# A two-layer graph kernel: scores of a block row from its diagonal block on, the other blocks as PE transposes of kept score blocks

## The chip, the cores and the metric

The kernel runs on one core of a Trainium2 chip. A core has a matrix engine (TensorE, in the profile PE for matmuls and PEld for the weight loads that precede them), a vector engine (VectorE, DVE), a scalar engine (ScalarE, ACT), GpSimd (POOL) and a sync engine (SP) that issues DMAs here. Each engine runs its own instruction stream in order and they meet at semaphores. The metric is the device time of one execution in microseconds (us). Before the change the median of three runs is 462.99 us (461.92 to 464.63).

## The reference, cut to what matters

Eight batches (B = 8) of N = 1024 nodes with H = 128 features, all f32, and an adjacency matrix `adj` of 0 and 1 per batch.

```python
# layer 0
u = einsum('bnh,bmh->bnm', x, x) / 128 ** 0.5      # symmetric in n and m
scores = softmax(u, axis=-1)
delta = scores * adj
att = delta / (sum(delta, axis=2, keepdims=True) + 1e-10)
# att is split in the parts right of, on and left of the diagonal, each with its own projection
ctx = att_left @ (x @ Wl.T + bl) + att_self @ (x @ Ws.T + bs) + att_right @ (x @ Wr.T + br)
x = layernorm(x + relu(ln_w * norm(ctx) + ln_b))
# layer 1
d = (sum(adj, axis=-1) + 1e-5) ** -0.5
x = layernorm(x + (d[:, :, None] * adj * d[:, None, :]) @ (x @ W1) + b1)
```

`u` is symmetric: block (i, j) of 128 x 128 is the transpose of block (j, i).

## The kernel before, in words

A batch is cut into NB = 8 block rows of P = 128 nodes (HB = 4 is half of them). Per batch and block row i the work goes round the engines like this:

- PE `scores(b, i)`: the block row of `u`, 128 x 1024, into the PSUM buffer `ps_u` (two banks, one buffer for all block rows). x is held as a rounded part `xT_hi` and a rest `xT_lo` (dtype float32r), and `split_matmul` multiplies hi by hi, hi by lo and lo by hi, each over 512 columns, twice: six matmuls (lines 403 to 405, printed with `ps_u` as output).
- DVE `row_max` (line 1060) reduces `ps_u` to the negative row maximum; ACT `exps` (line 805) writes exp(u - max) from `ps_u` to `d_rows` in SBUF. `scores` of the next block row waits for `exp_done`, since it overwrites `ps_u`.
- DVE `masked` (line 1067) multiplies with the adjacency rows; PE `turn_d` (line 463) makes eight 128 x 128 transposes into `ps_d`; ACT `d_out` (line 812) copies them to `dT`; POOL `masks` (line 1405) cuts the diagonal block; PE `context_far` and `context_near` (lines 478 and 484) multiply with the projected rows `h_sum`.

Beside them per batch: eight projections of x on PE (`project`, 384 columns each, lines 403 to 405 with `ps_m` as output) with a bias add on DVE (line 263); DVE 32 x 32 transposes of the adjacency (`turn_blocks`) that DMAs from SP complete into `aT`; the second layer's products `gather` (line 498, 512 columns, into `ps_y`), a copy `y_out` to `yT` on ACT (line 850) and `second_product` (line 510); the layer norms, spread over DVE, POOL and ACT. `x1b` holds the residual rows with the bias of layer 1 and `fin` the result rows before the store. ACT sums adjacency rows with a copy to `junk` whose accumulator is kept (line 818).

The order of the work on each engine is written out by hand, instruction by instruction: one list for batches 0 and 1 (`first_batches`), one for batches 2 to 6 (`batch(b, p)`, with p = b - 1 whose layers 0 and 1 finish inside batch b) and one for batch 7 and the end (`last_batches`). No planner or pool decides anything. Batch b's scores calls stand among the contexts, projections and gathers of batches b and p.

Of the kernel before, what the change touches and what calls it, by code (L numbers as in the profile page):

```python
# [11 lines left out]
P = 128  # L12
# [13 lines left out]
def two_layer_graph_kernel(nc, x, adj, Wl, bl, Ws, bs, Wr, br, ln_w, ln_b, W1, b1, out):  # L26
# [10 lines left out]
    with ExitStack() as ctx:  # L37
# [6 lines left out]
        def sem(name):  # L44
            return ctx.enter_context(nc.semaphore(name))
# [15 lines left out]
        x_turned = sb("x_turned", [P, NQ, NB, Q])  # L61
        h_sum = sb("h_sum", [P, 2, NB, 3 * H])
# [13 lines left out]
        junk_d = sb("junk_d", [P, P], mybir.dt.bfloat16)  # L76
# [45 lines left out]
        exp_done = sem("exp_done")  # L122
        d_ready = sem("d_ready")
# [90 lines left out]

        def y_bank(b, i0, i1):
# [52 lines left out]
        def _(sp):  # L268
# [58 lines left out]
            def first_batches(b, p):  # L327
# [26 lines left out]
                next_a(b, 1)
                next_a(b, 2)
                move_rows(b)
                next_a(b, 3)
                move_blocks(b, 0)
                next_a(b, 4)
                store(p, 0, HB)  # L360
                next_a(b, 5)
                next_a(b, 6)
                store(p, HB, NB)

            def batch(b, p):
# [12 lines left out]
                next_a(b, 5)
                store(p, HB, NB)
                next_a(b, 6)  # L380

            def last_batches(b, p):

                move_blocks(p, 1)
                next_a(p, 7)
# [7 lines left out]

# [6 lines left out]
        def _(pe):  # L400
# [34 lines left out]
            def scores(b, i):  # L435
# [68 lines left out]
            def second_product(b, i0, i1):  # L504
# [4 lines left out]
                for i in range(i0, i1):  # L509
                    last = pe.matmul(o_bank(b, i0, i1)[:, i - i0, :], yT[:, i * P:(i + 1) * P],  # L510
# [3 lines left out]
            def first_batches(b, p):  # L514
# [80 lines left out]
                gather(p, 0, HB, 3, 4)  # L595
# [12 lines left out]
                gather(p, 0, HB, 4, 8)  # L608
# [18 lines left out]
            def batch(b, p):  # L627
# [31 lines left out]
                gather(p, 0, HB, 3, 4)  # L659
# [9 lines left out]
                gather(p, 0, HB, 4, 8)  # L669
# [6 lines left out]
                gather(p, HB, NB, 1, 4)  # L676
# [3 lines left out]
                gather(p, HB, NB, 4, 8)  # L680
# [8 lines left out]
            def last_batches(b, p):  # L689
# [29 lines left out]
                gather(p, 0, HB, 2, 4)  # L719
# [17 lines left out]
                gather(p, 0, HB, 4, 6)  # L737
                gather(p, 0, HB, 6, 8)
# [15 lines left out]
                gather(p, HB, NB, 2, 4)  # L754
                gather(p, HB, NB, 4, 6)
                gather(p, HB, NB, 6, 8)
                m_read_o(p, 0, HB)
                second_product(p, HB, NB)
                gather(b, 0, HB, 0, 4)
                gather(b, HB, NB - 2, 0, 2)  # L760
                gather(b, NB - 2, NB, 0, 2)
                gather(b, 0, HB, 4, 6)
                gather(b, 0, HB, 6, 8)
# [3 lines left out]
                gather(b, HB, NB - 2, 3, 4)  # L767
                gather(b, HB, NB - 2, 4, 6)
                gather(b, HB, NB - 2, 6, 8)
                gather(b, NB - 2, NB, 2, 4)  # L770
                second_product(b, HB, NB - 2)
                gather(b, NB - 2, NB, 4, 6)
                gather(b, NB - 2, NB, 6, 8)
                second_product(b, NB - 2, NB)

# [31 lines left out]

# [811 lines left out]
```

## Time and profile before

| | |
|---|---|
| runs, median (lowest to highest) | 462.99 us (461.92 to 464.63) |
| span of the profiled execution | 461.6 us (the profile has no other time for it) |
| PE / PEld busy | 444.2 / 357.7 us |
| DVE / ACT / POOL busy | 388.8 / 296.8 / 310.9 us |
| score matmuls on `ps_u`, L403 + L404 + L405, x372 | 154.1 us busy |
| transposes L463, x512 | 66.4 us busy |
| exp on ACT, L805, x62 | 68.9 us busy, 50.3 us idle before them |

Matmuls are pipelined: the time of one (mean 394 ns for a 512-column score matmul) is longer than the distance to the next one's start, so it is the distance between starts that tells what it costs in a row. The number in brackets at a row's end is the idle time of the engine before it and what ended it.

### The profile page before, as it was taken

To read this page: it belongs to the slowest core of one execution; us is meant where nothing else is said; L and a number is where in the kernel's file an instruction comes from. 1 tells how busy PE (TensorE), PEld (TensorE's weight loads), DVE (VectorE), ACT (ScalarE), POOL (GpSimd) and SP (SyncE) were. 2 spreads that over 40 slices of the span, in tenths; PEclk is the share of its full clock that TensorE was granted. 3 is DMA by queue.
4 is the path that set the end of the run, shared out by engine and by line. 5 is a ranking of instruction groups with operands and counts; after the bars stand their busy time and mean duration, and the time that the engine had idled before them with its cause. 6 is when DMAs were issued, how large, how long until landed. Compare 5 with 4: busy or idle time off the path is not lost. (4 is left out here: it accounts for less than half of the span.)

```text
span 461.6 us, 8799 instructions
## 1 busy us (share of the span) xinstructions
PE 444.2 (96%) x2663; PEld 357.7 (77%) x2663; DVE 388.8 (84%) x696; ACT 296.8 (64%) x611; POOL 310.9 (67%) x364
## 2 busy tenths in 40 slices
PE   6899999999999999999999999999999999999974
PEld 4689879589776988679786797769887697879453
DVE  2998899979999889988899889998899887988625
ACT  2768767666666766765767657676676667677320
POOL 2115767379758867588675886588675967889662
PEclk9999999999999999999999999999999999999988
DMA  5836758285773889259881779528893493367721
GB/s 176 288 139 176 236 132 266 58 210 182 168 225 95 207 259 243 83 143 260 201 241 39 186 229 227 189 74 212 253 220 129 120 240 127 69 161 175 176 62 45
DMA packets 68878, 79.88 MB, mean 173 GB/s; under 512 B 7232, under 2 KB 60608, under 8 KB 68832
## 3 DMA queue, kind: packets, MB, share of 16 engines
q1 hardware_dynamic: 68768, 79.26, 62.1%
q8 instruction: 22, 0.36, 0.4%
q14 instruction: 24, 0.20, 0.1%
q0 software_dynamic: 64, 0.07, 0.0%
HBM read 38.40 MB, written 4.19 MB: 92 GB/s over the span
## 5 line engine op out<-in xcount | busy, mean ns | idle before, releaser
L478 PE MATMUL ps_c<-h_sum,dT 128*128 128x128 f32 x896 | 110.5, 275 | 0.9 <-issue 0.9
L478 PEld LDWEIGHTS ps_c<-h_sum,dT 128*128 128x128 f32 x896 | 106.9, 192 | 4.6 <-issue 4.0
L1405 POOL TENSOR_TENSOR dM<-dT,parts 128x384 f32<-128x384 f32 x64 | 67.9, 1063 | 58.2 <-ACT junk_d L826 31.7
L498 PE MATMUL ps_y<-aT,x1p 128*128 128x512 f32 x224 | 104.3, 592 | 0.0
L805 ACT ACTIVATE d_rows<-ps_u,nmax 128x1024 f32<-128x1024 f32 x62 | 68.9, 1112 | 50.3 <-DVE nmax L1060 50.2
L812 ACT ACTIVATE dT<-ps_d 128x1024 f32<-128x1024 f32 x64 | 65.3, 1021 | 40.8 <-PE ps_d L463 35.1
L1060 DVE TENSOR_REDUCE nmax<-ps_u 128x1 f32<-128x1024 f32 x62 | 75.3, 1215 | 16.6 <-PE ps_u L405 15.8
L1067 DVE CUSTOM_DVE_ANT_0 d_rows<-d_rows,a_rows 128x1024 f32<-128x1024 f32 x64 | 84.8, 1326 | 0.4 <-ACT d_rows L805 0.4
L1074 DVE STREAM_TRANSPOSE a_blk<-a_rows 128x1024 f32<-128x1024 f32 x64 | 77.4, 1228 | 0.8 <-DMA a_rows<-in_adj_dram 0.8
L818 ACT ACTIVATE junk<-a_rows 128x1024 bf16<-128x1024 f32 x64 | 67.1, 1048 | 0.3
L463 PE MATMUL ps_d<-parts,d_rows 128*128 128x128 f32 x512 | 66.4, 273 | 0.0
L463 PEld LDWEIGHTS ps_d<-parts,d_rows 128*128 128x128 f32 x512 | 58.6, 141 | 6.2 <-issue 4.4
L498 PEld LDWEIGHTS ps_y<-aT,x1p 128*128 128x128 f32 x224 | 39.7, 190 | 29.9 <-issue 29.4
L403 PE MATMUL ps_u<-xT_hi 128*128 128x512 f32 x124 | 56.6, 457 | 0.5
L405 PE MATMUL ps_u<-xT_hi,xT_lo 128*128 128x512 f32 x124 | 48.9, 394 | 0.0
L404 PE MATMUL ps_u<-xT_lo,xT_hi 128*128 128x512 f32 x124 | 48.6, 392 | 0.0
L263 DVE TENSOR_TENSOR h_sum<-ps_m,bias_bc 128x384 f32<-128x384 f32 x64 | 35.3, 551 | 14.7 <-PE ps_m L405 12.4
L484 PEld LDWEIGHTS ps_c<-h_sum,dM 128*128 128x128 f32 x256 | 36.0, 191 | 4.5 <-issue 2.9
L484 PE MATMUL ps_c<-h_sum,dM 128*128 128x128 f32 x256 | 38.9, 274 | 0.0
L255 POOL TENSOR_SCALAR fin<-fin,power_f,shift_f 128x128 f32<-128x128 f32 x56 | 36.2, 659 | 0.3
L1421 POOL TENSOR_TENSOR power_c<-var_c,minus_half 128x4 f32<-128x4 f32 (+1 forms) x17 | 22.2, 1304 | 20.1 <-DVE nmean_c L1119 20.1
L403 PE MATMUL ps_m<-wT_hi,xT_hi 128*128 128x384 f32 x64 | 28.4, 444 | 5.0 <-DVE h_sum L263 3.7
(95 smaller groups left out, 692.1 us busy)
## 6 DMA issues: line engine op xcount, KB each, us to landing
a_rows<-in_adj_dram SPq DMA_DIRECT2D x64, 512.0 KB, 4.5
aT<-a_blk SPq DMA_DIRECT2D x224, 128.0 KB, 2.9
x_rows<-in_x_dram SPq DMA_DIRECT2D x8, 512.0 KB, 4.5
a_rows<-a_blk SPq DMA_DIRECT2D x32, 128.0 KB, 2.4
out_dram<-fin SPq DMA_DIRECT2D x15, 256.0 KB, 2.6
x_turned<-x_blk SPq DMA_DIRECT2D x96, 32.0 KB, 1.9
out_dram<-fin SPq DMA_DIRECT2D x2, 128.0 KB, 1.8
fin<-in_L_gnn_Wl_dram SPq DMA_DIRECT2D x1, 64.0 KB, 3.4
```

Of the source, the lines that this page charges most:

```text
L403: pe.matmul(o, hi_l, hi_r, start=True, stop=False)
L463: last = pe.transpose(ps_d[:, j, :], d_rows[:, g % 3, j * P:(j + 1) * P], ident)
L478: pe.matmul(ps_c[:, c_place(b, i), :], dT[:, i % 2, j, :], h_sum[:, b % 2, j, k * H:(k + 1) * H], start=t == 0, stop=False)
L484: last = pe.matmul(ps_c[:, c_place(b, i), :], dM[:, i % 2, k, :], h_sum[:, b % 2, i, k * H:(k + 1) * H], start=False, stop=k == 1)
L498: last = pe.matmul(y_bank(b, i0, i1), gathered(b)[:, j, :], turned(b)[:, i0:i1, :, j, :].rearrange("p i q c -> p (i q) c"), start=j == 0, ...
L805: act.activation(d_rows[:, g % 3, :], u_bank(b, i), ACT.Exp, bias=nmax[:, i % 2:i % 2 + 1], accum_out=zsum[:, i:i + 1]).then_inc(exp_done, 1)
L812: act.activation(dT[:, i % 2, :, :], ps_d[:, :, :], ACT.Copy).then_inc(dt_out, 1)
L818: act.activation(junk[:, :], a_rows[:, i, :], ACT.Copy, accum_out=deg[:, i:i + 1])\
L1060: dve.tensor_reduce(nmax[:, i % 2:i % 2 + 1], u_bank(b, i), AX.X, ALU.max, negate=True)\
L1067: dve.tensor_tensor_reduce(out=d_rows[:, g % 3, :], in0=d_rows[:, g % 3, :], in1=a_rows[:, i, :], scale=1.0, scalar=0.0, op0=ALU.mult, op1 ...
L1074: dve.transpose(a_blk[:, i, :, :, :], a_rows[:, i, :].rearrange("p (j m c) -> p m j c", m=NQ, c=Q))\
L1405: pool.tensor_tensor(dM[:, i % 2, :, :], dT[:, i % 2, i, :].rearrange("p (a c) -> p a c", a=1).to_broadcast([P, 3, P]), parts[:, :, :], AL ...
```

## The change

In batch 0 nothing changes for the scores. From batch 1 on, `scores(b, i)` computes only the columns from block i on with `split_matmul`; blocks 0 to i - 1 of the row are PE transposes of blocks (j, i), j < i, which ACT has copied from `ps_u` to a new SBUF buffer `kept` when block row j stood there. The copy is `keep(b, j)` (one or two `Copy` activations), placed directly behind `exps(b, j)` for j = 0 to 6. `scores(b, i)` waits for the `keep` of the row before in addition to `exp_done`. To make room in SBUF, `yT` holds half of the rows, `x1b` lives in `fin` (in the last batch in a part of `h_sum`), and the junk outputs are 8 bits wide. Some neighbouring gather calls are merged into one call. All other orders are unchanged.

```diff
+        kept = sb("kept", [P, HB, HB, P])
-        yT = sb("yT", [P, N])
+        yT = sb("yT", [P, HB, P])
-        x1b = sb("x1b", [P, NB, H])
-        junk = sb("junk", [P, N], mybir.dt.bfloat16)
+        junk = sb("junk", [P, N], mybir.dt.float8e4)
...
+        def halves(b):
+            return b == 0
+
+        def kept_before(b, i):
+            return (NB - 1) * (b - 1) + i
+
+        def kept_parts(i):
+            if i == 0:
+                return [(kept[:, 0:2, :, :].rearrange("p a c m -> p (a c) m")[:, 1:NB, :], 1, NB)]
+            if i < HB - 1:
+                return [(kept[:, 0, 0:2, :] if i == 1 else kept[:, 0, 2:3, :], i + 1, HB), (kept[:, i + 1, :, :], HB, NB)]
+            if i == HB - 1:
+                return [(kept[:, 0, :, :], HB, NB)]
+            return [(kept[:, 1:NB - i, i - HB, :], i + 1, NB)]
...
             def scores(b, i):
...
-                for k in range(2):
-                    c = slice(k * HALF, (k + 1) * HALF)
-                    last = split_matmul(u_bank(b, i)[:, c], hi[:, s], lo[:, s], hi[:, c], lo[:, c])
+                if not halves(b) and i:
+                    pe.wait_ge(u_kept, kept_before(b, i))
+                j0 = 0 if halves(b) else i
+                for c in (slice(j0 * P, HALF), slice(max(j0 * P, HALF), N)):
+                    if c.start < c.stop:
+                        last = split_matmul(u_bank(b, i)[:, c], hi[:, s], lo[:, s], hi[:, c], lo[:, c])
+                for j in range(j0):
+                    last = pe.transpose(ps_u[:, j * P:(j + 1) * P], kept_block(j, i), ident)
                 last.then_inc(u_ready, 1)
...
+            def keep(b, i):
+                act.wait_ge(nmax_ready, NB * b + i + 1)
+                for v, j0, j1 in kept_parts(i):
+                    last = act.activation(v, ps_u[:, j0 * P:j1 * P].rearrange("p (j c) -> p j c", c=P), ACT.Copy)
+                last.then_inc(u_kept, 1)
...
             def rows_with_bias(b, i0, i1):
                 n, blk = NB * b + i1, slice(i0, i1)
                 pool.wait_ge(x_power, n)
-                wait(pool, o_read, NB * (b - 1) + HB * ((i1 - 1) // HB + 1))
+                if b == B - 1:
+                    pool.wait_ge(ctx_done, NB * b)
+                else:
+                    wait(pool, fin_free[i0 // HB], 16 * b)
+                x1b = rows_x1b(b)
```

On PE, block row 3 of a middle batch before the change (the projection in front of it fills `ps_m`, L498 with `ps_y` is a gather):

```order
L498 MATMUL ps_y<-aT,x1p 128x512
L403 MATMUL ps_u<-xT_hi 128x512 [waits exp_done,xt_split]
L404 MATMUL ps_u<-xT_lo,xT_hi 128x512
L405 MATMUL ps_u<-xT_hi,xT_lo 128x512
L403 MATMUL ps_u<-xT_hi 128x512
L404 MATMUL ps_u<-xT_lo,xT_hi 128x512
L405 MATMUL ps_u<-xT_hi,xT_lo 128x512
L403 MATMUL ps_m<-wT_hi,xT_hi 128x384 [waits xt_split,h_added]
```

The same place after the change (L433 to L435 are the old L403 to L405, L479 are the transposes of kept blocks, `parts` holds the identity, L533 is the gather):

```order
L533 MATMUL ps_y<-aT,x1p 128x512
L433 MATMUL ps_u<-xT_hi 128x128 [waits u_kept,exp_done,xt_split]
L434 MATMUL ps_u<-xT_lo,xT_hi 128x128
L435 MATMUL ps_u<-xT_hi,xT_lo 128x128
L433 MATMUL ps_u<-xT_hi 128x512
L434 MATMUL ps_u<-xT_lo,xT_hi 128x512
L435 MATMUL ps_u<-xT_hi,xT_lo 128x512
L479 MATMUL ps_u<-parts,kept 128x128 x3
L433 MATMUL ps_m<-wT_hi,xT_hi 128x384 [waits xt_split,h_added]
```

The first half of the row shrinks to one block of 128 columns and three transposes follow the second half; the first score matmul waits for `u_kept` too, and nothing else moves.

On ACT, block rows 0 and 1 of the same batch before the change (L812 is `d_out`, L826 the sum of the diagonal, L818 the adjacency row sum):

```order
L812 ACTIVATE dT<-ps_d 128x1024 [waits dt_tr,ctx_done]
L805 ACTIVATE d_rows,zsum<-ps_u,nmax 128x1024 [waits c_sum,dt_tr,nmax_ready]
L826 ACTIVATE junk_d,ddiag<-dM 128x128 [waits self_done,diag_done,mask_done] x2
L805 ACTIVATE d_rows,zsum<-ps_u,nmax 128x1024 [waits c_sum,dt_tr,nmax_ready]
L818 ACTIVATE junk,deg<-a_rows 128x1024 [waits a_in0,deg_added,deg_done]
```

And after it (L844, L831, L859 and L850 are the same four, L837 is `keep`):

```order
L844 ACTIVATE dT<-ps_d 128x1024 [waits dt_tr,ctx_done]
L831 ACTIVATE d_rows,zsum<-ps_u,nmax 128x1024 [waits c_sum,dt_tr,nmax_ready]
L837 ACTIVATE kept<-ps_u 128x896 [waits nmax_ready]
L859 ACTIVATE junk_d,ddiag<-dM 128x128 [waits self_done,diag_done,mask_done] x2
L831 ACTIVATE d_rows,zsum<-ps_u,nmax 128x1024 [waits c_sum,dt_tr,nmax_ready]
L837 ACTIVATE kept<-ps_u 128x256 [waits nmax_ready]
L837 ACTIVATE kept<-ps_u 128x512
L850 ACTIVATE junk,deg<-a_rows 128x1024 [waits a_in0,deg_added,deg_done]
```

One or two copies stand behind each exp and push what follows on ACT back.

## Rows read from the trace of the kernel before

**Rows 1.** The page, busy time of each engine, share of the span.

```profile
PE 444.2 (96%) x2663; PEld 357.7 (77%) x2663; DVE 388.8 (84%) x696; ACT 296.8 (64%) x611; POOL 310.9 (67%) x364
```

**Rows 2.** By stretch: length, busy PE, PEld, DVE, ACT, POOL, then PE clock, DMA.

```profile
42.00:101.40 59.40, 58.75 (x371) 48.30 (x370) 53.95 (x95) 41.77 (x87) 38.84 (x41) 1.00 0.64 180
264.40:318.70 54.30, 54.24 (x331) 43.89 (x330) 48.01 (x86) 36.83 (x77) 39.46 (x45) 1.00 0.67 187
```

**Rows 3.** Timeline, PE, 264.3 to 286 (batch 5): start, duration, instruction.

```profile
270.29 0.39 PE L403 MATMUL ps_u<-xT_hi 128*128 128x512 f32 x1
...
271.68 0.60 PE L484 MATMUL ps_c<-h_sum,dM 128*128 128x128 f32 x4
...
274.74 0.39 PE L403 MATMUL ps_u<-xT_hi 128*128 128x512 f32 x1
...
279.92 0.40 PE L404 MATMUL ps_u<-xT_lo,xT_hi 128*128 128x512 f32 x1
...
281.07 0.33 PE L403 MATMUL ps_m<-wT_hi,xT_hi 128*128 128x384 f32 x1
...
281.59 1.03 PE L463 MATMUL ps_d<-parts,d_rows 128*128 128x128 f32 x8
282.46 1.02 PE L498 MATMUL ps_y<-aT,x1p 128*128 128x512 f32 x2
...
283.50 0.34 PE L404 MATMUL ps_m<-wT_lo,xT_hi 128*128 128x384 f32 x1
...
283.85 1.02 PE L498 MATMUL ps_y<-aT,x1p 128*128 128x512 f32 x2
...
285.24 0.39 PE L404 MATMUL ps_u<-xT_lo,xT_hi 128*128 128x512 f32 x1
```

**Rows 4.** Timeline, 286 to 300, ACT's exp of block row 4, PE's scores of 5.

```profile
290.46 1.11 ACT L805 ACTIVATE d_rows<-ps_u,nmax 128x1024 f32<-128x1024 f32 x1
...
293.08 0.40 PE L404 MATMUL ps_u<-xT_lo,xT_hi 128*128 128x512 f32 x1
```

**Rows 5.** Timeline, ACT, 264.3 to 286, the exps of block rows 0 to 3.

```profile
268.86 1.11 ACT L805 ACTIVATE d_rows<-ps_u,nmax 128x1024 f32<-128x1024 f32 x1
...
273.14 1.11 ACT L805 ACTIVATE d_rows<-ps_u,nmax 128x1024 f32<-128x1024 f32 x1 [2.20 <-DVE nmax L1060]
...
277.58 1.11 ACT L805 ACTIVATE d_rows<-ps_u,nmax 128x1024 f32<-128x1024 f32 x1 [0.66 <-DVE nmax L1060]
...
283.58 1.11 ACT L805 ACTIVATE d_rows<-ps_u,nmax 128x1024 f32<-128x1024 f32 x1 [0.93 <-DVE nmax L1060]
284.59 0.19 ACT L805 ACTIVATION_READ_ACCUMULATOR d_rows<-ps_u,nmax 128x1 f32 x1
```

**Rows 6.** Groups by form: count, busy us, mean ns, idle before us.

```profile
L478 PE MATMUL ps_c<-h_sum,dT 128*128 128x128 f32 x896 | 110.5, 275 | 0.9 <-issue 0.9
...
L850 ACT ACTIVATE yT<-ps_y 128x512 f32<-128x512 f32 x15 | 9.0, 597 | 27.2 <-issue 20.1 <-PE ps_y L498 7.1
...
L850 ACT ACTIVATE yT<-ps_u 128x256 f32<-128x256 f32 x2 | 0.8, 383 | 6.1 <-PE ps_u L498 6.1
```

**Rows 7.** Timeline, 60 to 67 (batch 1): exp of block row 3, second score matmul of 4.

```profile
63.57 1.10 ACT L805 ACTIVATE d_rows<-ps_u,nmax 128x1024 f32<-128x1024 f32 x1
...
65.72 0.39 PE L404 MATMUL ps_u<-xT_lo,xT_hi 128*128 128x512 f32 x1
```

**Rows 8.** Timeline, 376 to 394 (batch 7): exps of 0 and 2, scores of 1, 3.

```profile
376.92 1.12 ACT L805 ACTIVATE d_rows<-ps_u,nmax 128x1024 f32<-128x1024 f32 x1 [2.46 <-DVE nmax L1060]
...
378.34 0.48 PE L403 MATMUL ps_u<-xT_hi 128*128 128x512 f32 x1
...
387.18 1.11 ACT L805 ACTIVATE d_rows<-ps_u,nmax 128x1024 f32<-128x1024 f32 x1 [0.68 <-DVE nmax L1060]
...
388.63 0.39 PE L403 MATMUL ps_u<-xT_hi 128*128 128x512 f32 x1
```

**Rows 9.** Timeline, PE, 408 to 462, the last batch's gather behind its moves.

```profile
440.59 2.74 PE L498 MATMUL ps_u<-a_rows,h_sum 128*128 128x256 f32 x8 [2.24 <-DMA a_rows<-a_blk]
```

More of the change, by code:

```diff
@@ L658, in batch @@
                 project(b, 7)
-                gather(p, 0, HB, 3, 4)
+                gather(p, 0, HB, 3, HB)
                 scores(b, 4)
@@ L668, in batch @@
                 turn_d(b, 3)
-                gather(p, 0, HB, 4, 8)
+                gather(p, 0, HB, HB, NB)
                 scores(b, 6)
@@ L675, in batch @@
                 turn_d(b, 4)
-                gather(p, HB, NB, 1, 4)
+                gather(p, HB, NB, 1, HB)
                 context_far(b, 3)
@@ L817, in degree @@
                 act.wait_ge(a_in[i], 16 * (b + 1))
-                act.activation(junk[:, :], a_rows[:, i, :], ACT.Copy, accum_out=deg[:, i:i + 1])\
+                act.activation(junk[:, :], a_rows[:, i, :], ACT.Copy, accum_out=deg[:, i:i + 1],
+                               saturate=False)\
                    .then_inc(deg_done, 1)
@@ L848, in y_out @@
                 act.wait_ge(y_done, NB * b + i1)
-                wait(act, o_ready, NB * (b - 1) + i1)
-                act.activation(yT[:, i0 * P:i1 * P], y_bank(b, i0, i1), ACT.Copy).then_inc(yT_ready, i1 - i0)
+                wait(act, o_ready, NB * b + (HB if i0 >= HB and b < B - 1 else 0))
+                if b == B - 1 and i0 >= HB:
+                    act.wait_ge(u_ready, NB * B)
+                act.activation(y_place(b, i0, i1), y_bank(b, i0, i1).rearrange("p (j c) -> p j c", c=P), ACT.Copy)\
+                   .then_inc(yT_ready, i1 - i0)
             def first_batches(b, p):
@@ L885, in first_batches @@
                 exps(b, 0)
+                keep(b, 0)
                 degree(p, 7)
@@ L891, in first_batches @@
                 exps(b, 1)
+                keep(b, 1)
                 d_out(p, 7)
@@ L895, in first_batches @@
                 exps(b, 2)
+                keep(b, 2)
                 norm_x(p, 0, HB)
@@ L899, in first_batches @@
                 exps(b, 3)
+                keep(b, 3)
                 norm_c(p, HB, NB)
@@ L903, in first_batches @@
                 exps(b, 4)
+                keep(b, 4)
                 degree(b, 2)
@@ L911, in first_batches @@
                 exps(b, 5)
+                keep(b, 5)
                 degree(b, 3)
@@ L916, in first_batches @@
                 exps(b, 6)
+                keep(b, 6)
                 diagonal(b, 4)
@@ L933, in batch @@
                 exps(b, 0)
+                keep(b, 0)
                 diagonal(p, 6)
@@ L936, in batch @@
                 exps(b, 1)
+                keep(b, 1)
                 degree(b, 0)
@@ L939, in batch @@
                 exps(b, 2)
+                keep(b, 2)
                 d_out(b, 0)
@@ L942, in batch @@
                 exps(b, 3)
+                keep(b, 3)
                 degree(b, 1)
@@ L948, in batch @@
                 exps(b, 4)
+                keep(b, 4)
                 norm_x(p, HB, NB)
                 exps(b, 5)
+                keep(b, 5)
                 d_out(b, 3)
@@ L956, in batch @@
                 exps(b, 6)
+                keep(b, 6)
                 d_out(b, 4)
@@ L975, in last_batches @@
                 exps(b, 0)
+                keep(b, 0)
                 d_out(p, 7)
@@ L980, in last_batches @@
                 exps(b, 1)
+                keep(b, 1)
                 d_out(b, 0)
@@ L983, in last_batches @@
                 exps(b, 2)
+                keep(b, 2)
                 diagonal(b, 0)
@@ L987, in last_batches @@
                 exps(b, 3)
+                keep(b, 3)
                 norm_c(p, HB, NB)
@@ L992, in last_batches @@
                 exps(b, 4)
+                keep(b, 4)
                 d_out(b, 3)
@@ L997, in last_batches @@
                 exps(b, 5)
+                keep(b, 5)
                 d_out(b, 4)
@@ L1001, in last_batches @@
                 exps(b, 6)
+                keep(b, 6)
                 norm_c(b, 0, HB)
```

113 lines of the change are left out of this document (60 added, 53 removed).

## The prediction

> **What bounds the kernel now.** I read the engines' busy times first: PE is busy for 444.2 of 461.6 us, DVE for 388.8, ACT for 296.8 [rows 1]. Busy time of PE counts overlapping matmuls, so the second view is the table by stretch: in one middle batch of 54.30 us PE is busy 54.24, DVE 48.01, ACT 36.83, at a TensorE clock of 1.00 [rows 2]. The third is the timeline of that middle batch (b = 5), where I look at the distance between starts, which is what a matmul costs when another follows. The reader is to see that nearly everywhere PE starts an instruction where the interval of the previous one ends, so less work for PE is time won. But at the single score buffer ps_u the slack is thin: the scores of block i+1 may start only when the exp of block i has read the buffer.
>
> I write S0 to S7 for the eight scores calls of a batch. A score matmul behind a gather or a context is recorded early, so there I take as the real start the second matmul's start less 0.23. S1 starts at 270.29, S2 at 274.74, S3 at 279.69, S4 at 285.01 [rows 3], S5 at 292.85 [rows 4]. The exps before them end at 269.97, 274.25, 278.69, 284.69 [rows 5] and 291.57 [rows 4]. Before S4 stand two gather matmuls of 0.43 each (282.46 to a real 283.33 for the two before), started at 283.85, so PE is free at 284.71, yet S4 starts at 285.01 [rows 3]. That is a wait, and it gives the shortest distance from the end of an exp to scores: 0.32, of which 0.09 is the accumulator read that ends at 284.78 [rows 5]. Against "exp end + 0.32" the slack is 0.00 for S1, 0.17 for S2, 0.68 for S3, 0.00 for S4 and 0.96 for S5; S6, S7 and the next S0 have more.
>
> **The change part by part.** *Removed and added on PE.* Six 512-column score matmuls take 1.39 (270.29 to 271.68), 0.231 each; three 384-column ones of the projection take 0.52 (281.07 to 281.59), 0.173 each; so 0.46 ns per column, and 0.115 for 256; eight transposes take 0.87 (281.59 to 282.46), 0.109 each [rows 3]. A call costs 1.39 now. Afterwards S1 is 3 x 0.173 + 3 x 0.231 + 0.109 = 1.32, S2 is 0.35 + 0.69 + 0.22 = 1.26, S4 0.69 + 0.44 = 1.13, S5 0.52 + 0.55 = 1.06, S6 0.35 + 0.65 = 1.00. S3 and S7 hold three 128-column score matmuls each, and no row shows one of that kind. In proportion to columns it would be 0.058. The other end is a plain f32 matmul of 128 columns, which PE splits into two instructions (half of the x896, [rows 6]), each 0.109 or a little more, so 0.22. I take 0.173, the nearest row of the same kind, since nothing shows this kind cheaper: S3 0.52 + 0.69 + 0.33 = 1.54, S7 0.52 + 0.76 = 1.28. The changes are S1 -0.07, S2 -0.13, S3 +0.15, S4 -0.26, S5 -0.33, S6 -0.39, S7 -0.11: 1.14 less work per batch, 8.0 us over seven batches if nothing waits.
>
> *Added on ACT, and the added wait.* keep(b, i) stands right behind exps(b, i) on ACT, and the scores of i+1 wait for it; queued behind them is PE's whole stream, for which DVE and ACT then wait. A copy out of PSUM takes 0.597 for 512 columns and 0.383 for 256 [rows 6], so 0.92 for 896, 0.49 for 384, 0.28 for 128, and two in a row overlap by about 0.09 (the accumulator read is recorded at 284.59, before the exp ends at 284.69 [rows 5]). keep thus takes 0.92, 0.89, 0.78, 0.60, 0.49, 0.38, 0.28 for i = 0 to 6. It starts where the exp ends and has no accumulator read of 0.09 behind it, so PE's release moves by 0.83, 0.80, 0.69, 0.51, 0.40, 0.29, 0.19. In a middle batch:
> S0 to S1: no slack, +0.83.
> S1 to S2: chain -0.07 + 0.80, slack 0.17: +0.56.
> S2 to S3: chain -0.13 + 0.69, under the slack of 0.68, so PE's own -0.12.
> S3 to S4: chain +0.15 + 0.51, no slack: +0.66.
> S4 to the next S0: slack enough for 0.40, 0.29 and 0.19 on top of the shorter calls, so PE's own -0.26 - 0.33 - 0.39 - 0.11 = -1.09.
> Sum +0.84 per batch: 1.98 of new waits against 1.14 less work. Batches 2 to 6 run alike: 5 x 0.84 = +4.2.
>
> *Batch 1.* It has another order and later exps matter less. The tightest place is S4: its exp ends at 64.67, its real start is 65.49, a slack of 0.50 [rows 7]. I get -0.07, +0.03 and +0.17 for S1 to S3 and -1.09 for the rest: -0.96. DVE is busy 53.95 of 59.40 there, but PE 58.75 [rows 2], so PE still bounds it.
>
> *Batch 7.* S1 and S3 start 0.30 and 0.34 after their exps [rows 8], which is no slack: +0.83 and +0.56. S2 and S4 have room (-0.07, +0.15), and S5 to S7 take PE's saving as far as their slack goes: -0.11, -0.33, -0.27, and S7 itself -0.11. Sum +0.65. The tail hangs on S7: the second product behind it frees DVE for the last turns, and the moves behind those end the wait of 2.24 at 440.59 [rows 9]; so it shifts as a whole.
>
> *Priced at nothing.* Merging gathers removes nothing from PE; one of them (j = 4 to 7 of the last batch) asks for two later blocks of x1p, which follow at once; at worst it costs some tenths once. x1b moved into fin waits for a store of the batch before, issued a good third of a batch earlier; the half-size yT waits for a second product that stands before the next gather in PE's order. For the fp8 junk no row exists; if that output were slower by 0.1, or faster, it falls into the 17 us that ACT idles per batch [rows 2].
>
> Sum: 4.2 - 0.96 + 0.65 = +3.9 on the span of 461.6, so 465.5. The profile gives no time beside the span; the median of the runs, 462.99, lies 1.35 above it and the lowest run 0.3. On the median: **466.9 us**.
>
> **Rivals.** *A: narrow score matmuls are paced like the other 128-wide instructions, 0.109.* S3 and S7 get 0.19 cheaper each: 0.39 per middle batch, 0.35 in batches 1 and 7, -2.65 in all: 464.2. For it: transposes show this pace, and a matmul must load its weights whatever streams. Against it: those rows are of another kind. The Trainium skill, TensorE: Matmul & The Clock Gate, section LDWEIGHTS, gives a load of 128 weight columns as 107 ns, independent of what streams; by that rule A's time would be the outcome, and the trace's 0.109 agrees with it.
> *B: narrow score matmuls lose their fast pace and cost the f32 price, 0.22.* +0.144 in S3 and S7, 14 times: +2.0, 468.9. For it: 512 f32 columns cost two instructions of 0.43 [rows 3] where this kind takes one of 0.231, so the pace is a privilege that a shape may lose. Against it: 384 columns show no sign of that.
> *C, the other side: faster.* The new waits bite less than read and the saved work shows. If PE resumes 0.2 sooner after each wait (three in each of six batches, -3.6) and the narrow matmuls cost 0.058 (-0.34 each, 13 times, -4.4), the time is 459. It decides where the new waits of a batch fall under its saved work, 1.98 against 1.14 to 1.83. Against it: 0.32 is a measured distance.
> *D: ACT runs late.* The copies add 3.8 us per batch to ACT's 36.83. If that pushes copies of dT or the masks behind them past PE's need by 1 us a batch: 473. Against it: ACT idles 17 us per batch [rows 2], most of it waiting for PE and DVE.
> The Trainium skill, same page, Part 4: PE-mode transpose, holds that transposes do not count as activity for the clock, which speaks against putting transposes in the place of matmuls. Eight transposes per block run already at a clock of 1.00 [rows 2, 3], so the trace does not bear it out. Were the clock halved around the new ones, 28 more of 0.109 in each of seven batches would cost 21 us, 488; I give this 0.01, within D.
>
> **How the numbers follow.** Forecast 0.28, A 0.27, B 0.25, C 0.12, D 0.08. About 0.5% (2.3 us) is what a measurement of this kernel can tell from no change. Slower by more (above 465.3): most of the forecast, B, D and a fifth of A, 0.64. Within it: the rest of A, some of the forecast and of C, 0.26. Faster: 0.10. The range, 461.5 to 471, holds A, B and the forecast with 2 us for misread slacks, and leaves out most of C and D.
>
> **What would show it.** After the change PE waits for ACT's copy to kept before S1, S2 and S4, by 0.83, 0.63 and 0.51 us; the distance between starts of 128-column score matmuls (0.058, 0.109, 0.173 or 0.22) decides between the cases; S5 to S7 start without a wait and that part comes 1.1 us closer; a middle batch lasts 55.1 instead of 54.3. No wait at S1, or a middle batch under 54 us, would make the prediction wrong, and so would waits of PE on dT or masks.

## The result: slower by half a per cent, and the profile after

The changed kernel takes 465.87 us (median of 20 runs, 465.08 to 467.87), the kernel before in the same comparison 463.40 (20 runs, 461.91 to 466.01): a ratio of 1.0055 with a 95% interval of 1.0042 to 1.0067, so 2.5 us more. The forecast was 466.9, or 3.9 more. The profiled execution of the changed kernel spans 464.0 us against 461.6.

The first part of the page of the changed kernel (busy time of each engine, its share of the span, its instructions) answers to [rows 1].

```profile
PE 437.1 (94%) x2775; PEld 355.0 (76%) x2775; DVE 391.0 (84%) x696; ACT 321.4 (69%) x674; POOL 307.9 (66%) x364
```

PE is busy 7.1 us less and ACT 24.6 more, and yet the span is 2.4 longer. The table by stretch (length, busy time of PE, PEld, DVE, ACT and POOL with their instruction counts, granted clock, share of the DMA engines, GB/s) shows batch 1 and the middle batch 5 of the changed kernel, from the real start of their S0 to that of the next batch's S0, and answers to [rows 2].

```profile
42.66:101.63 58.97, 57.74 (x387) 48.10 (x386) 54.17 (x95) 45.26 (x96) 39.58 (x41) 1.00 0.65 179
265.92:320.69 54.77, 53.31 (x347) 43.47 (x346) 48.67 (x86) 40.36 (x86) 38.54 (x45) 1.00 0.66 183
```

The middle batch lasts 54.77 instead of 54.30, and PE, which was idle for only 0.06 of it, now idles 1.46 at an unchanged clock of 1.00. Its timeline on PE shows the new waits, and answers to [rows 3].

```profile
272.48 0.41 PE L433 MATMUL ps_u<-xT_hi 128*128 128x384 f32 x1 [0.56 <-ACT kept L837]
272.73 0.34 PE L434 MATMUL ps_u<-xT_lo,xT_hi 128*128 128x384 f32 x1
...
277.46 0.35 PE L433 MATMUL ps_u<-xT_hi 128*128 128x256 f32 x1 [0.35 <-ACT kept L837]
277.65 0.28 PE L434 MATMUL ps_u<-xT_lo,xT_hi 128*128 128x256 f32 x1
277.77 0.28 PE L435 MATMUL ps_u<-xT_hi,xT_lo 128*128 128x256 f32 x1
277.89 0.40 PE L433 MATMUL ps_u<-xT_hi 128*128 128x512 f32 x1
...
282.26 0.32 PE L433 MATMUL ps_u<-xT_hi 128*128 128x128 f32 x1
282.42 0.27 PE L434 MATMUL ps_u<-xT_lo,xT_hi 128*128 128x128 f32 x1
282.54 0.27 PE L435 MATMUL ps_u<-xT_hi,xT_lo 128*128 128x128 f32 x1
282.64 0.45 PE L433 MATMUL ps_u<-xT_hi 128*128 128x512 f32 x1
...
288.08 0.47 PE L433 MATMUL ps_u<-xT_hi 128*128 128x512 f32 x1 [0.55 <-ACT kept L837]
288.39 0.39 PE L434 MATMUL ps_u<-xT_lo,xT_hi 128*128 128x512 f32 x1
```

S1 (272.48), S2 (277.46) and S4 (288.08) wait for ACT's copy, S3 (282.26) doesn't. Three 128-column score matmuls start at 282.26, 282.42 and 282.54 and the next instruction at 282.64: 0.10 to 0.12 apart once the row runs, as 256 columns are (277.65, 277.77, 277.89). ACT's timeline at block row 0 of that batch, which answers to [rows 5]:

```profile
270.33 1.11 ACT L831 ACTIVATE d_rows<-ps_u,nmax 128x1024 f32<-128x1024 f32 x1
271.33 0.20 ACT L831 ACTIVATION_READ_ACCUMULATOR d_rows<-ps_u,nmax 128x1 f32 x1
271.42 0.92 ACT L837 ACTIVATE kept<-ps_u 128x896 f32<-128x896 f32 x1
```

The copy starts with the exp's last 0.02 still running and ends at 272.34; S1 starts really (second matmul less 0.17, since the first is of 384 columns) at 272.56, 0.22 later. In all ACT is busy 24.6 us longer (321.4 - 296.8). The waits of PE over the whole kernel (total, times, longest):

```profile
PE ps_u L433 <- ACT kept L837: 8.7, 18, 0.6
PE ps_u L533 <- DMA a_rows<-a_blk: 1.6, 1, 1.6
PE ps_y L533 <- ACT h_sum L865: 1.5, 1, 1.5
```

18 waits for `kept` make 8.7 us. A wait in this list counts from the recorded end of the matmul before, so it is shorter than the delay that the distance between starts shows (0.56 against 0.81 at S1). The last row is one wait that the kernel before doesn't have; it belongs to a merged gather in the last batch.

Where the 2.4 us of the spans sit, by real starts of the same calls in both traces: before batch 1, where the scores don't differ, +0.55; batch 1 -0.41; batches 2 to 6 +0.40, +0.46, +0.46, +0.46, +0.44, together +2.22; batch 7 from S0 to S7 +0.81 (39.82 to 40.63); from there to the end -0.77 (47.70 to 46.93). The first of these is no effect of the change: the real start of batch 1 lies at 42.66 here, at 42.11 before, and between 42.2 and 44.4 in the profiles of the experiments, which compute batch 0 alike.

The end of batch 7 behind S7 is where a small difference hides two large ones. The rows on PE that follow a wait there, of the changed kernel; the first answers to [rows 9].

```profile
442.90 1.99 PE L533 MATMUL ps_u<-a_rows,h_sum 128*128 128x256 f32 x8 [1.63 <-DMA a_rows<-a_blk]
446.40 3.67 PE L533 MATMUL ps_y<-a_rows,h_sum 128*128 128x512 f32 x8 [1.51 <-ACT h_sum L865]
450.86 1.13 PE L545 MATMUL ps_m<-w_sb,yT 128*128 128x128 f32 x8 [0.35 <-issue]
```

The table by stretch of the kernel before, behind its wait of 2.24:

```profile
441.70:445.20 3.50, 3.50 (x8) 2.07 (x7) 0.00 (x0) 0.88 (x2) 2.99 (x7) 0.51 0.02 5
445.20:448.40 3.20, 2.94 (x8) 1.14 (x6) 0.00 (x0) 0.60 (x1) 2.72 (x6) 1.00 0.25 72
```

and of the changed kernel, behind its wait of 1.63 and across the one of 1.51:

```profile
442.90:446.40 3.50, 1.99 (x8) 1.46 (x9) 1.44 (x7) 1.75 (x4) 2.15 (x6) 1.00 0.09 26
446.40:450.80 4.40, 4.10 (x10) 1.79 (x10) 0.00 (x0) 0.60 (x1) 4.02 (x9) 1.00 0.00 0
```

Before, the granted clock fell to 0.51 of full speed (that is the 1.2 GHz level) for 3.5 us after the wait of 2.24; the same eight gather matmuls of 256 columns that take 1.99 in the changed kernel took 2.74 [rows 9]. In the changed kernel the clock stays at 1.00, but PE waits 1.51 more in front of the merged gather. From the end of the DMA wait to the second product the two need 7.90 (440.59 to 448.49) and 7.96 us (442.90 to 450.86): the two effects cancel. The second product of the kernel before:

```profile
448.49 1.13 PE L510 MATMUL ps_m<-w_sb,yT 128*128 128x128 f32 x8 [0.35 <-issue]
```

### The profile page after: what moved, and what is told of

Its sections match the earlier page's. It is cut to its first block and busy times, and to the rows that moved or that the text cites. A ratio compares the mean times of both kernels' runs of the same rounds, so it can differ in the third digit from the quotient of the medians.

```text
span 464.0 us, 9068 instructions
## 1 busy us (share of the span) xinstructions
PE 437.1 (94%) x2775; PEld 355.0 (76%) x2775; DVE 391.0 (84%) x696; ACT 321.4 (69%) x674; POOL 307.9 (66%) x364
## 5 line engine op out<-in xcount | busy, mean ns | idle before, releaser
L533 PE MATMUL ps_y<-aT,x1p 128*128 128x512 f32 x224 | 104.4, 593 | 0.0
L831 ACT ACTIVATE d_rows<-ps_u,nmax 128x1024 f32<-128x1024 f32 x62 | 69.0, 1112 | 47.8 <-DVE nmax L1117 47.5
L844 ACT ACTIVATE dT<-ps_d 128x1024 f32<-128x1024 f32 x64 | 65.6, 1024 | 31.3 <-PE ps_d L498 26.6
L1124 DVE CUSTOM_DVE_ANT_0 d_rows<-d_rows,a_rows 128x1024 f32<-128x1024 f32 x64 | 86.5, 1352 | 0.4 <-ACT d_rows L831 0.4
L850 ACT ACTIVATE junk<-a_rows 128x1024 fp8e4<-128x1024 f32 x64 | 67.4, 1053 | 0.3
L498 PE MATMUL ps_d<-parts,d_rows 128*128 128x128 f32 x512 | 66.4, 273 | 0.0
L533 PEld LDWEIGHTS ps_y<-aT,x1p 128*128 128x128 f32 x224 | 39.5, 190 | 29.7 <-issue 29.7
L498 PEld LDWEIGHTS ps_d<-parts,d_rows 128*128 128x128 f32 x512 | 58.4, 141 | 5.0 <-issue 4.4
L433 PE MATMUL ps_u<-xT_hi 128*128 128x512 f32 (+3 forms) x96 | 40.1, 418 | 8.8 <-ACT kept L837 8.7
L519 PEld LDWEIGHTS ps_c<-h_sum,dM 128*128 128x128 f32 x256 | 34.6, 191 | 3.5 <-issue 2.9
L433 PEld LDWEIGHTS ps_u<-xT_hi 128*128 128x128 f32 x96 | 18.1, 189 | 23.1 <-issue 22.5
L433 PE MATMUL ps_m<-wT_hi,xT_hi 128*128 128x384 f32 x64 | 29.0, 454 | 5.4 <-DVE h_sum L294 4.1
L435 PE MATMUL ps_u<-xT_hi,xT_lo 128*128 128x512 f32 (+3 forms) x96 | 33.8, 352 | 0.0
L434 PE MATMUL ps_u<-xT_lo,xT_hi 128*128 128x512 f32 (+3 forms) x96 | 33.7, 352 | 0.0
```

The costliest lines, as they stand in the source:

```text
L433: pe.matmul(o, hi_l, hi_r, start=True, stop=False)
L498: last = pe.transpose(ps_d[:, j, :], d_rows[:, g % 3, j * P:(j + 1) * P], ident)
L519: last = pe.matmul(ps_c[:, c_place(b, i), :], dM[:, i % 2, k, :], h_sum[:, b % 2, i, k * H:(k + 1) * H], start=False, stop=k == 1)
L533: last = pe.matmul(y_bank(b, i0, i1), gathered(b)[:, j, :], turned(b)[:, i0:i1, :, j, :].rearrange("p i q c -> p (i q) c"), start=j == 0, ...
L831: act.activation(d_rows[:, g % 3, :], u_bank(b, i), ACT.Exp, bias=nmax[:, i % 2:i % 2 + 1], accum_out=zsum[:, i:i + 1]).then_inc(exp_done, 1)
L844: act.activation(dT[:, i % 2, :, :], ps_d[:, :, :], ACT.Copy).then_inc(dt_out, 1)
```

## The experiments

My theory when they began: the saved PE work is worth about 1.5 us per batch, the waits for the copies take back more, and all else in the change costs nothing. The rivals: the rest of the change has a price, or the copies cost by ACT's load and not by PE's wait.

**e1: the rest of the change alone.**

```diff
         def halves(b):
-            return b == 0
+            return True
...
             def keep(b, i):
+                return
```

> The change without kept copies and without transposes: all scores full width in every batch, but yT, x1b and junk placed as in the change and the gathers merged. Theory (the time comes from the copies' wait against saved PE work): this part is worth nothing but the merged gather of the last batch, which waited 1.5 us for x1p and started 0.5 us later against the start of its half than before; so 463.4 to 464.0, ratio 1.000 to 1.001 to the kernel before. Rival (the rest of the change carries a part of the loss: the profile after starts batch 0 0.56 us late and batch 7's tail waits): 464.5 to 465, ratio 1.0025 or more.

Measured: 463.25 us against 463.66, ratio 1.0002 (0.9987 to 1.0017), middle batches 54.30. So half yT, x1b in `fin`, the narrower junk and the merged gathers make no difference together. I read that as "each is free" and was wrong by two terms, which e11 below separates: its trace has the wait of 1.55 in front of the merged gather, and no fallen clock.

**e2: no copies and no wait for them.**

```diff
-                if not halves(b) and i:
-                    pe.wait_ge(u_kept, kept_before(b, i))
...
-                    last = pe.transpose(ps_u[:, j * P:(j + 1) * P], kept_block(j, i), ident)
+                    last = pe.transpose(ps_u[:, j * P:(j + 1) * P], ident, ident)
...
             def keep(b, i):
+                return
```

> Leaves out the copies to kept and the wait for them; the transposes read the identity in place of kept blocks, so the left part of each score row is not the reference's. It prices the saved PE work alone. Theory: a 128-column score matmul is paced at 0.11, a call S1 to S7 gets 0.07, 0.13, 0.05, 0.26, 0.33, 0.39 and 0.31 shorter, 1.5 us per batch, middle batch 52.8, in all about -10 us: 453.4, ratio 0.978. Rival (DVE or the exp chain takes over as the bound once PE is quicker, so that the saving was never there): not more than half, 458 or above, ratio 0.989 or more.

Measured: 456.01 us, ratio 0.9851 (0.9829 to 0.9872), between the two expectations. Middle batches last 53.24 to 53.37, so the saved work brings 1.05 a batch, less than the 1.5 that the narrow matmuls' pace gives. The steps behind S0, S2, S6 and S7 move as they should (the one behind S7 by 0.26 of 0.31); S5 to S6 does not shorten (5.74 against 5.70), though S5 has 0.32 less to do. The timeline of PE in e2 behind S5:

```profile
289.12 0.71 PE L477 MATMUL ps_u<-parts 128*128 128x128 f32 x5
289.67 1.04 PE L496 MATMUL ps_d<-parts,d_rows 128*128 128x128 f32 x8
290.82 1.53 PE L531 MATMUL ps_y<-aT,x1p 128*128 128x512 f32 x3
```

and that of ACT there:

```profile
289.03 1.65 ACT L864 ACTIVATE x1p<-c_rows,shift_x,scale_x 128x128 f32<-128x128 f32 x4 [1.63 <-POOL shift_x L1509]
```

The transposes of `turn_d`, eight at 0.109 from 289.67, are through at 290.54, and the gather starts at 290.82: it asks for the half of x1p that ACT's norm writes until 290.68, and that norm waited 1.63 for POOL. The layer norm's chain over DVE, POOL and ACT lies just under PE's order here. In the changed kernel the waits at S1, S2 and S4 give that chain its time, and there S5 to S6 does shorten, 5.70 to 5.38.

**e3: the copies alone.** All scores in full width, copies and waits as in the change.

```diff
-                j0 = 0 if halves(b) else i
+                j0 = 0
```

> Copies and the wait as in the change, but scores at full width and no transposes (same result). It prices the wait alone. Theory: waits of 0.83, 0.63, 0.01 and 0.51 before S1 to S4 of a middle batch, 1.98 per batch, 1.8 in batch 7 and 0.2 in batch 1 (0.9 if the delay of S3 seen there belongs to the copies): +12 to 12.6, about 475.7, ratio 1.026. Rival (ACT's extra 3.8 us per batch costs something beyond the three waits): 479 or more, ratio 1.034.

Measured: 474.68 us, ratio 1.0256 (1.0230 to 1.0281), and 56.19 a middle batch, 1.89 more than before, where the forecast has 0.83 + 0.63 + 0.51 = 1.97 of waits. The wait before S1 in that batch (S0 starts at 273.11, S1 at 279.73), on PE:

```profile
279.65 0.47 PE L433 MATMUL ps_u<-xT_hi 128*128 128x512 f32 x1 [0.56 <-ACT kept L837]
```

**e4: short copies.** Every `keep` is one copy of 32 columns, so the waits stand and what PE waits for is short.

```diff
-                for v, j0, j1 in kept_parts(i):
-                    last = act.activation(v, ps_u[:, j0 * P:j1 * P].rearrange("p (j c) -> p j c", c=P), ACT.Copy)
+                for v, j0, j1 in kept_parts(i)[-1:]:
+                    last = act.activation(v[:, 0:1, 0:Q], ps_u[:, j0 * P:j0 * P + Q].rearrange("p (j c) -> p j c", c=Q), ACT.Copy)
```

> As the change, but each keep copies 32 columns only (one instruction) and the transposes read the identity, so the left part of a score row is not the reference's; the semaphore and the wait stay. Theory (length of the copy sets the wait): release 0.12 later than the exp's instead of 0.83, 0.80, 0.69, 0.51, so the middle batch is 53.1 and the time about 455.5, ratio 0.983. Rival (the wait for one more semaphore or one more instruction behind the exp costs by itself, whatever its length): little better than the change, 462 or more.

Measured: 457.71 us, ratio 0.9886 (0.9865 to 0.9907), with 53.34 to 53.63 a middle batch and 1.2 us of waits for `kept` in all. It is 1.7 above e2 in the median and 0.9 in the span (455.5 against 454.6), of which the middle batches explain 0.7; but it is 8 below the change. So it is the copies' duration that costs, not the second semaphore. Since short copies also spare ACT most of the work, e4 alone does not tell PE's wait from ACT's load; e6 does. I expected 455.5, for I had not yet seen the chain of e2. The table by stretch (columns as above) of batch 5 in e2, from S0 to the next S0:

```profile
260.63:313.89 53.26, 53.07 (x347) 43.65 (x346) 48.46 (x86) 36.82 (x77) 39.54 (x45) 1.00 0.70 191
```

and of the same batch in e3:

```profile
273.11:329.30 56.19, 54.73 (x331) 43.79 (x330) 47.83 (x86) 40.38 (x86) 38.47 (x45) 1.00 0.67 184
```

Saved work 54.30 - 53.26 = 1.04, new waits 56.19 - 54.30 = 1.89, the change 54.77: 0.38 less than 54.30 with both (55.15). S5 to S6 alone makes 0.36 of that (5.74 in e2, 5.38 in the change), the saving that counts only with the waits.

**e6: wait by PSUM bank.** The copies and their semaphore are split by bank, the first bank's copy goes first, scores start in a bank once that one is free, and the transposes of rows 4 to 7 stand ahead of the wait.

```diff
...
+                if j0 < HB:
+                    kept_before(0)
+                    fresh(j0 * P, HALF)
+                    if j0:
+                        turn(0, j0)
+                    kept_before(1)
+                    last = fresh(HALF, N)
+                else:
+                    turn(0, min(HB, i - 1))
+                    kept_before(1)
+                    last = fresh(j0 * P, N)
+                    last = turn(min(HB, i - 1), i) if i > min(HB, i - 1) else last
...
```

> The change with the wait split by PSUM bank: each of the two parts of a keep has its own semaphore (row 0's copy is cut in 384 and 512 columns), scores of rows 1 to 3 fill bank 0 first and wait for the second part only before bank 1, rows 4 to 7 make their transposes of older rows before they wait. Same result. Theory (a wait as long as the copy stands between an exp and the next scores): waits of 0.40, about 0.05 and 0.18 in place of 0.8, 0.6 and 0.5, middle batch 53.5 to 53.7, time 458.5 to 459.5, ratio 0.990. Rival (the loss is ACT's extra work, or the saving of rows 1 to 7 is mostly given back elsewhere): 463 or more, ratio 0.999 or more.

Measured: 459.46 us, ratio 0.9909 (0.9895 to 0.9923). PE's first work of a row then hides the second half of the copy, and no wait for `kept` is long enough to stand in the list of PE's waits. The first half of row 0's copy still shows in the starts: S0 to S1 takes 6.23 in batch 5, against 5.83 before and 6.64 in the change, and that batch lasts 53.74. ACT is busy 40.31 in it, as in the change (40.36): so it is not ACT's load that costs, but where PE waits for it.

**e9: rows 1 to 3 in full.** As e6, but rows 1 to 3 are computed in full width, rows 4 to 7 use kept blocks, and rows 0 to 3 keep only the four blocks of the second bank.

```diff
-                return [(kept[:, 0, 0:2, :] if i == 1 else kept[:, 0, 2:3, :], i + 1, HB), (kept[:, i + 1, :, :], HB, NB)]
+                return [(kept[:, i + 1, :, :], HB, NB)]
...
-                j0 = 0 if halves(b) else i
+                j0 = 0 if halves(b) or i < HB else i
```

> As the split wait, but only the blocks of rows 0 to 3 times columns 4 to 7 and of rows 4 to 6 are kept: rows 1 to 3 are computed at full width (they saved 0.07, 0.13 and 0.05), their keep copies 512 columns of bank 1 only, and PE fills bank 0 meanwhile. Same result. Theory: PE needs 0.69 for bank 0 from exp end + 0.32 and the copy releases bank 1 at exp end + 0.83, so S1, S2, S3 wait for nothing, S4 for 0.18; rows 4 to 7 keep their saving: middle batch 53.2 to 53.4, time about 457, ratio 0.986. Rival (any copy between exp and scores costs its length, bank or not): +0.5 per copy in S1, S2 and S4, middle batch 54.6, 463 or above.

Measured: 457.5 us, ratio 0.9868 (0.9855 to 0.9882). On PE at S4 of batch 5:

```profile
280.56 1.02 PE L546 MATMUL ps_y<-aT,x1p 128*128 128x512 f32 x2
281.65 0.52 PE L479 MATMUL ps_u<-parts,kept 128*128 128x128 f32 x3
282.05 0.50 PE L428 MATMUL ps_u<-xT_hi 128*128 128x512 f32 x1
282.38 0.39 PE L429 MATMUL ps_u<-xT_lo,xT_hi 128*128 128x512 f32 x1
```

Three transposes (281.65) run where the changed kernel waited, and the fresh scores follow at most 0.17 behind them (real start 282.38 - 0.23 = 282.15; three transposes at 0.109 from 281.65 are through at 281.98). The middle batches take 53.40 to 53.69.

**e10: e9 with one merged gather cut again.**

```diff
-                gather(b, 0, HB, HB, NB)
+                gather(b, 0, HB, HB, NB - 2)
+                gather(b, 0, HB, NB - 2, NB)
```

> The same as the late rows, and the merged gather of the last batch (j = 4 to 7) cut in two again, so that j = 4, 5 needn't wait for the last two blocks of x1p. Theory: PE idled 1.5 us there after the change and the start was 0.5 us later against the half's start than before; two matmul pairs (4 x 0.43) move ahead of the wait, so 0.5 to 1.5 us less than the late rows, ratio about 0.984. Rival (the end hangs on x1p of the last two blocks either way, as those matmuls come last in the group): no difference, below 0.3 us.

Measured: 455.59 us, ratio 0.9832 (0.9814 to 0.9851), which beats the kernel before by 1.7%: 8.1 us below its median in the same comparison (463.69). That is 1.9 less than e9, more than I expected of a term that the prediction had put at nothing, so I tried it in the change itself.

**e11: the change with that gather cut.** The same edit as e10's, nothing else.

> The changed kernel with one of its merged gathers cut in two again: gather(b, 0, HB, HB, NB) of the last batch becomes blocks 4 and 5, then 6 and 7; nothing else differs. Theory (the merged call waits for the second half of x1p, which ACT's norm of x writes last, and PE idles 1.51 us in front of it): the first six matmuls' worth of work of that call runs under the wait, the wait at 446.40 goes, all else is alike: 465.9 - 1.5 = 464.4, with every batch as long as in the change (54.76 in a middle batch). Rival (PE's wait is only passed on, since the last turns and the DMA behind them end the kernel): 465.5 to 466.0.

Measured: 463.88 us against 463.83, ratio 1.0009 (0.9992 to 1.0027); the changed kernel has 1.0055. All batches are as long as in the change (54.74 to 54.78 in batches 2 to 5). The rows on PE that answer to the changed kernel's 442.90, 446.40 and 450.86:

```profile
443.42 1.99 PE L533 MATMUL ps_u<-a_rows,h_sum 128*128 128x256 f32 x8 [1.60 <-DMA a_rows<-a_blk]
445.25 3.64 PE L533 MATMUL ps_y<-a_rows,h_sum 128*128 128x512 f32 x8
449.68 1.13 PE L545 MATMUL ps_m<-w_sb,yT 128*128 128x128 f32 x8 [0.35 <-issue]
```

From the DMA wait's end to the second product it takes 6.26 us instead of 7.96. So the merge costs 1.7 us, and without it the change is no slower than the kernel before as that one seems to run most of the time, with a fallen clock at the end (more on that below). By the medians of the two comparisons the cut brings 2.0 (465.87 to 463.88). It also explains e1: 7.99 there from 440.19 to 448.18, with full clock and merged gather, against 7.90 before with the fallen clock and the cut gather.

**e12: who delays batch 1.** Batch 1 gained only 0.41; S2 to S3 took 5.58 there instead of 4.89, with a wait for DVE's bias add. In e2 it took 4.72, so the copies do it. ACT's timeline of the changed kernel in batch 1:

```profile
47.67 0.91 ACT L837 ACTIVATE kept<-ps_u 128x896 f32<-128x896 f32 x1
48.47 1.06 ACT L850 ACTIVATE junk<-a_rows 128x1024 fp8e4<-128x1024 f32 x1
...
49.51 1.64 ACT L865 ACTIVATE c_rows<-c_rows,shift_c,power_c 128x128 f32<-128x128 f32 x4
```

POOL's of the same stretch:

```profile
49.70 1.31 POOL L1494 TENSOR_SCALAR vdeg<-deg 128x4 f32<-128x4 f32 x1 [1.01 <-ACT junk L850]
51.09 1.04 POOL L1496 TENSOR_TENSOR dinv<-vdeg,minus_half 128x4 f32<-128x4 f32 x1
52.10 1.28 POOL L278 TENSOR_TENSOR c_rows<-c_rows,lnw_bc 128x512 f32<-128x512 f32 x1
```

DVE's, the bias add that PE waits for:

```profile
57.61 0.54 DVE L294 TENSOR_TENSOR h_sum<-ps_m,bias_bc 128x384 f32<-128x384 f32 x1
```

and PE's, the projection behind it:

```profile
58.21 0.44 PE L433 MATMUL ps_m<-wT_hi,xT_hi 128*128 128x384 f32 x1 [0.58 <-DVE h_sum L294]
```

The copy (47.67) delays the adjacency row sum (48.47), POOL's degree step waits 1.01 for that, its products with the norm's weights stand behind it (52.10), DVE's add of x and the norm's sums follow, and behind these in DVE's order the bias add. The edit lets the row sum go first:

```diff
                 exps(b, 0)
-                keep(b, 0)
                 degree(p, 7)
+                keep(b, 0)
                 norm_c(p, 0, HB)
```

> The changed kernel with two neighbouring steps of ACT in batch 1 exchanged: degree(p, 7) stands ahead of keep(b, 0) instead of behind it. Theory (the copy delays the adjacency row sum, POOL's degree power waits for that, behind it stand POOL's two products with the norm's weights, DVE's add of x, the bias add, and PE's projection at 58.21): in batch 1 the distance S2 to S3 falls from 5.58 to 4.7 to 5.0 and PE no longer waits 0.58 for the bias add, while S0 to S1 grows from 6.38 to about 7.1, because the copy, and with it PE's release, comes 1.05 us later with 0.3 us of slack. Rival (it is ACT's norm of the contexts, not the row sum, that passes the delay on): S2 to S3 stays at 5.5 to 5.6. Batches 2 to 6 stay at 54.76. In the time, 465.6 to 466.3 by the theory and 466.3 to 467 by the rival.

Measured: 465.93 us, ratio 1.0056 (1.0036 to 1.0075). S2 to S3 is 4.75, S0 to S1 7.18 instead of 6.38, and all middle batches stay at 54.75 to 54.78. The theory's chain is shown. POOL's degree step in e12:

```profile
48.95 0.24 POOL L1494 TENSOR_SCALAR vdeg<-deg 128x4 f32<-128x4 f32 x1 [0.21 <-ACT junk L850]
```

and PE's projection in e12, the row that started at 58.21 after a wait of 0.58:

```profile
58.24 0.42 PE L433 MATMUL ps_m<-wT_hi,xT_hi 128*128 128x384 f32 x1
```

POOL starts 0.75 earlier and the projection waits for nothing, though it starts no earlier: the time is the same because the wait only moves to S1.

Not tried: the copy running beside DVE's row maximum instead of behind the exp. Whether that would take the copy off the round trip is open.

## Why the prediction was nearly right, point by point

**The waits held.** Forecast: +0.83, +0.56 and +0.66 at S0 to S1, S1 to S2 and S3 to S4, and PE's own -0.12 between S2 and S3. Measured in batch 5: +0.81, +0.54, +0.53 and -0.19 (only the third of the forecast holds the narrow price, in S3; with A's price it is +0.47). Forecast durations of the copies of 896 and 512 columns 0.92 and 0.597, measured means 0.914 and 0.594. The rule "end of ACT's read + 0.32, less the 0.09 of the accumulator read" gave 0.23, and S1 starts 0.22 after its copy. S5 to S7 start without a wait in the middle batches, and S4 to the next S0 came to -1.23 against -1.09 (-1.28 with A's price for S7).

**The narrow matmul was mis-sized.** The term that was wrong is "I take 0.173, the nearest row of the same kind". It measured 0.10 to 0.12, which was rival A: 0.39 less a batch turns +0.84 into +0.45, and batch 5 measured +0.46. With it the forecast would have been 464.2, further from the measured 465.87 than 466.9 was: that the stated number came so close is in part luck, one error standing against others. The nearest kind was the wrong neighbour: the 128-wide transposes had the same weight load and showed the pace. The Trainium skill, TensorE: Matmul & The Clock Gate, section LDWEIGHTS, has 107 ns for such a load; the trace agrees for these starts, and the rule that I set beside the sum was the better one.

**"Priced at nothing" held a real price.** The step "one of them asks for two later blocks of x1p, which follow at once; at worst it costs some tenths once" failed. It was 1.7 us (e11). The blocks do not follow at once. ACT's norm writes blocks 4 and 5 until 443.96 and blocks 6 and 7 until 446.26, 2.30 later:

```profile
443.08 0.88 ACT L865 ACTIVATE h_sum<-c_rows,shift_x,scale_x 128x128 f32<-128x128 f32 x2 [4.95 <-POOL shift_x L1510]
445.38 0.88 ACT L865 ACTIVATE h_sum<-c_rows,shift_x,scale_x 128x128 f32<-128x128 f32 x2 [1.42 <-POOL shift_x L1510]
```

In the cut form PE has the matmuls of blocks 4 and 5 for that time, four instructions of 0.43 us. I read the order and not the time at which each half of x1p is ready.

**The tail does not shift as a whole.** Its DMA wait was 0.6 shorter (2.24 to 1.63) and the clock that fell after it in the kernel before stayed up. That was worth 0.6 and 1.6 us for the changed kernel (1.6 is 7.90 - 6.26, the same work with the cut gather at either clock). I named [rows 9] and did not ask why eight 256-column matmuls took 2.74 there. The one profile of the kernel before can't say how often that happens, but every execution on record has its mean granted clock. Of the 47 of the kernel before that ran beside the experiments, 35 have 0.994 or less (median 463.94 us) and 12 have 0.996 or more (median 462.12): 1.8 us apart, and 3.5 us at 0.51 is 0.004 of the span. Of the changed kernel's 20 only 7 lie at 0.994 or less, of e1's 12 only 4; that also fits e1, which has the merge's 1.7 us and still measures 1.0002, where 1.0037 would be due without a gain of that size. Against the executions of the kernel before that kept their clock the change is slower by some 3.6 us, not 2.5 (an estimate: the median of its 11 executions at 0.996 or more is 465.74).

The mean does not tell where the clock fell. In the profiles of e3 and e11 it fell in batch 0 (0.50 from 16.5 to 19.5 and from 15.5 to 18.5), which is part of why their batch 1 starts late, at 44.38 and 43.22; in e3 that followed a wait of 2.18 of PE, in e11 one of 1.47, and e9 has a wait of 1.47 at the same place and kept its clock. So that the shorter DMA wait kept the clock up in the change is likely (it is 1.33 to 1.70 in the profiles of all nine experiments, and none of them falls there) but not shown by a run that varies that wait alone. Why the DMA wait is shorter is not settled; e1 (1.57) shows that it does not need the copies.

**Batch 1 was taken too lightly.** Forecast -0.96, and -1.31 with rival A's price; measured -0.41. The step "later exps matter less" looked at the exps alone. What was late was the row sum behind the copy (e12): rival D's mechanism, at one place, for 0.7 us.

**Batch 7:** forecast +0.65 up to and with S7's own -0.11, +0.30 with A's price, measured +0.81 from S0 to S7 and -0.25 from there to the second product, so +0.56. The miss is S6 to S7, +0.30 where -0.27 stood. The step that failed is "as far as their slack goes", which took S7's slack for enough. S7 waits there for the copy of row 6, on PE:

```profile
417.06 0.30 PE L433 MATMUL ps_u<-xT_hi 128*128 128x128 f32 x1 [0.48 <-ACT kept L837]
```

and DVE's row maximum of row 6, ahead of that copy's exp, in the change and in the kernel before:

```profile
414.30 1.21 DVE L1117 TENSOR_REDUCE nmax<-ps_u 128x1 f32<-128x1024 f32 x1
411.15 1.21 DVE L1060 TENSOR_REDUCE nmax<-ps_u 128x1 f32<-128x1024 f32 x1
```

It stands directly behind the norm's statistics in DVE's order and starts 3.21 after S6 here (411.09), 2.93 before (408.22). So less work in S6 does not bring the exp forward, and the copy comes on top. In e2, without copies, PE waits 0.36 for the exp at that place, and the step is +0.19.

**The sum.** On the spans, with A's price: 3.9 - 2.65 = +1.25. Add batch 1's 0.90, batch 7's 0.26, the tail's -0.6 - 1.6 + 1.7 = -0.5, and the 0.55 before batch 1 that is no effect of the change: 2.46, against 2.4 measured. The score part of the change, batches 1 to 7 with the tail left out, costs -0.41 + 2.22 + 0.56 = +2.4; that the whole measures about the same is the tail's cancelling. So the direction was right for the reason given. The change was forecast 1.4 us too large (3.9 against 2.5), because a price 2.65 too high stood against 1.2 of delays in batches 1 and 7 that I had not seen and the shift of the start. The time itself came out only 1.0 high, since the kernel before measured 0.4 more in this comparison (463.40) than the 462.99 that the sum started from.

**The clock** took no harm from 196 more transposes: 1.00 in the middle batch, 0.996 over the span. The Trainium skill, same page, Part 4: PE-mode transpose, says that the full clock does not engage for them. This trace shows no harm from them, but it is no test of that sentence: at most 14 transposes stand in a row here, 1.5 us between matmuls.

## What to carry to other kernels

Recomputing less can lose when what replaces it sits on the only buffer's round trip: count the copy that holds the buffer before the work that it saves, and let the consumer wait for the part that it overwrites first (e6, e9). A call merged for tidiness waits for the last of its inputs: look up when each input is ready, not whether it comes next. A row that takes longer than its twins is a question, in the tail above all: a change can win time there by shortening a wait that the clock fell behind, and hide a loss of its own.

## What was unexpected of the hardware

- A float32r matmul of 128 columns is followed by the next after 0.10 to 0.12 us, the same as one of 256 columns (0.12), against 0.173 for 384 and 0.231 for 512.
- One wait of 2.24 us was followed by a clock of 0.51 for 3.5 us; waits of 1.63 and 1.51 with 1.99 of matmuls between them were not (1.00). In batch 0 one of 1.47 was in e11 (0.50 for 3.0 us) and one of 1.47 was not in e9 (1.00): the same order of work can meet the fall in one execution and not in another.
- The 8-bit junk output changed nothing on ACT: the row sum over 1024 columns takes 1.048 in the mean with bf16 in the kernel before and 1.053 with fp8 after.
- PE started 0.22 to 0.23 us after the end of the ACT copy that it waited for.
